# TensorE's layer loop begins with the scores, and the waits of the groups behind them stand ahead of them

## What is computed

```python
def attn_layer(x, Wqkv, qs, ksc, Wo):            # 16 heads of 64, window of 32 tokens
    q, k, v = jnp.split(x @ Wqkv, 3, -1)         # after heads are split:
    q = l2norm(q) * qs; k = l2norm(k) * ksc
    q = q * cos * scale + rotate_half(q) * sin * scale
    k = k * cos / scale + rotate_half(k) * sin / scale
    sim = jnp.einsum('bhwie,bhwje->bhwij', bq, bk2) * 8.0   # own window and the one before
    attn = jax.nn.softmax(jnp.where(mask, -big, sim), -1)
    return jnp.einsum('bhwij,bhwje->bhwie', attn, bv2) @ Wo
for i in range(6):
    x = attn_layer(shift_tokens(x), ...) + x
    x = ffn_layer(shift_tokens(x), ...) + x      # layer norm, W1, a * gelu(gate), W2
```

## Time and profile before

| | us |
|---|---|
| median of three runs | 4279.43 |
| the profiled execution's own time | 4280.44 |
| its span | 4278.5 |
| PE busy | 3922.0 (92%) |
| DVE busy | 3477.7 (81%) |
| ACT busy | 3345.8 (78%) |
| POOL busy | 2759.5 (64%) |
| mean granted clock of TensorE | 0.965 of 2.4 GHz |

### The profile page before, as it was taken

How to read it: one execution, slowest core, us unless ns; L and a number is a source line. 1 busy time by engine, 2 the same in 40 slices (tenths; PEclk the granted TensorE clock), 3 DMA queues, 4 the chain that set the end, 5 groups by cost and what they waited for, 6 DMA issues and landing times. The chain is left out here.

```text
span 4278.5 us, 192301 instructions
## 1 busy us (share of the span) xinstructions
PE 3922.0 (92%) x73440; PEld 3294.1 (77%) x73441; DVE 3477.7 (81%) x6455; ACT 3345.8 (78%) x6195; POOL 2759.5 (64%) x3194
## 2 busy tenths in 40 slices
PE   6999779866778999999999999999999999999997
PEld 4555437644458888888888888888888888888886
DVE  6888475464568999999989999999999999999994
ACT  4777445543348998999989999899989999899995
POOL 3333146641466777777777777777777777777772
PEclk9999899987879999999999999999999999999999
DMA  4000046447111112211122111311122111221111
GB/s 169 1 0 0 16 137 216 157 139 292 53 46 48 48 47 65 63 47 48 47 77 57 44 46 46 84 50 48 47 68 60 46 48 47 78 57 47 47 44 39
DMA packets 155926, 290.43 MB, mean 68 GB/s; under 512 B 35600, under 2 KB 58256, under 8 KB 152080
## 3 DMA queue, kind: packets, MB, share of 16 engines
q1 hardware_dynamic: 147632, 271.29, 21.5%
q0 software_dynamic: 8192, 17.84, 1.4%
HBM read 87.68 MB, written 62.91 MB: 35 GB/s over the span
## 5 line engine op out<-in xcount | busy, mean ns | idle before, releaser
L2833 POOL TENSOR_TENSOR d_rc<-d_rc,d_rs 128x512 f32<-128x512 f32 x768 | 967.9, 1282 | 277.6 <-DVE d_rs L2900 230.5
L2403 PE MATMUL d_pair<-d_W_parts,d_xs_high 128*128 128x512 f32 x2304 | 782.9, 421 | 71.8 <-issue 37.8
L2843 POOL TENSOR_TENSOR d_rc<-d_rc,d_inv 128x1024 f32<-128x1024 f32 x384 | 723.8, 1906 | 112.0 <-DVE d_inv L2921 111.9
L2650 ACT ACTIVATE d_sq<-d_pair 128x512 f32<-128x512 f32 x768 | 455.5, 593 | 181.4 <-DVE d_rs L2900 118.4
L2900 DVE TENSOR_TENSOR d_rc<-d_pair,d_rot 128x512 f32<-128x512 f32 x768 | 524.2, 683 | 18.0 <-ACT d_sq L2650 11.9
L2900 DVE TENSOR_TENSOR d_rs<-d_pair,d_rot 128x512 f32<-128x512 f32 x768 | 522.1, 680 | 0.0
L2403 PEld LDWEIGHTS d_pair<-d_W_parts,d_xs_high 128*128 128x128 f32 x2304 | 389.9, 191 | 163.5 <-issue 101.9
L2403 PE MATMUL d_pair<-d_W_parts,d_xs_low 128*128 128x512 f32 x1152 | 458.7, 398 | 0.0
L2910 DVE TENSOR_REDUCE d_ss<-d_sq 128x16 f32<-128x1024 f32 x384 | 448.2, 1208 | 0.0
L2928 DVE TENSOR_REDUCE d_mx<-d_pair 128x16 f32<-128x1024 f32 x192 | 235.1, 1225 | 220.5 <-PE d_pair L2489 220.5
L2550 PEld LDWEIGHTS d_pair<-d_OT,d_Wo 128*128 128x128 f32 x3072 | 376.2, 193 | 18.4 <-issue 1.5
(11 more groups left out here) (395 smaller groups left out, 9829.5 us busy)
## 6 DMA issues: line engine op xcount, KB each, us to landing
d_VW<-d_V SPq DMA_DIRECT2D x768, 128.0 KB, 2.4
d_VW<-d_V SPq DMA_DIRECT2D x576, 64.0 KB, 2.0
projection_parts<-b_table SPq DMA_DIRECT2D x36, 512.0 KB, 5.5
d_W_parts<-projection_parts SPq DMA_DIRECT2D x36, 512.0 KB, 5.8
leaf_rows<-a_zeros SPq DMA_DIRECT2D x12, 1152.0 KB, 14.6
q_xrow<-leaf_rows SPq DMA_DIRECT2D x24, 576.0 KB
leaf_out<-q_yrow SPq DMA_DIRECT2D x24, 512.0 KB
b_table<-Wqkv_dram SPq DMA_DIRECT2D x36, 256.0 KB, 5.3
```

The source lines that it names most:

```text
L2403: mm = nc.tensor.matmul(target, x_part[:, t.par, :], W_parts[:, c, w_part, :].bitcast(F32R), start=n == 0, stop=n == 2)
L2650: nc.scalar.activation(sq[:, half, 512 * j:512 * j + 512], ps[:, j, :], ACT.Square).then_inc(s[f"s{qk}{j}_ready"], 1)
L2833: nc.gpsimd.tensor_tensor(own[:, :, a, :], own[:, :, a, :], other[:, :, 1 - a, :], ALU.add).then_inc(s[f"add{qk}_ready"], 1)
L2843: nc.gpsimd.tensor_tensor(heads(rc[:, t.par, half, :]), heads(rc[:, t.par, half, :]), inv[:, t.par, half, :].unsqueeze(2).to_broadcast([12 ...
```

## The change

The slot of TensorE is turned round: scores and attend move from its end to its beginning, one tile index later, so the sequence of groups stays the same except at two points. The first keys product now precedes the second queries product. And the loop's branch, which stood between attend and the products, now stands between `hidden_gate` and scores. All waits of attend, and of the two products behind it those for the weights and for `h_ready`, are put ahead of scores; `xs_split` stays with the first keys product and is dropped from queries 1 and keys 1, which now follow a group that has waited for it.

```diff
-                if t.first:
+                if t.first and what not in ("q1", "k0"):
                     pe.wait_ge(s_w[what], 16 * t.l + 16)
-                wait(pe, "xs_split", t)
+                if what not in ("q1", "k1"):
+                    wait(pe, "xs_split", t)
...
                 if j == 0:
-                    wait(pe, "h_ready", t, -7, HCH)
...
-            def scores(t):
-
-                if not t.live:
-                    return
-                wait(pe, "kt_ready", t)
-                wait(pe, "qt_ready", t)
-                wait(pe, "ot_ready", t, -2)
-                if t.edge:
-                    wait(pe, "sc_ready", t, -1)
+            def needs_of_next_groups(behind, ahead):
+
+                if ahead.live:
+                    if ahead.first:
+                        pe.wait_ge(s_w["k0"], 16 * ahead.l + 16)
+                        pe.wait_ge(s_w["q1"], 16 * ahead.l + 16)
+                    wait(pe, "h_ready", ahead, -7, HCH)
+                if behind.live:
+                    wait_spread(pe, behind)
+                    wait(pe, "pt_ready", behind)
                 pe.sem_inc(s["gate_pe"], 1)
+
+            def scores(t, behind, ahead):
+
+                if t.live:
+                    wait(pe, "kt_ready", t)
+                    wait(pe, "qt_ready", t)
+                    wait(pe, "ot_ready", t, -2)
+                    if t.edge:
+                        wait(pe, "sc_ready", t, -1)
+                needs_of_next_groups(behind, ahead)
+                if not t.live:
+                    return
...
-                wait_spread(pe, t)
-                wait(pe, "pt_ready", t)
-                pe.sem_inc(s["gate_pe"], 1)
...
             def slot(tile):
+                scores(tile(2), behind=tile(3), ahead=tile(0))
+                attend(tile(3))
+                keys(tile(0), 0)
                 queries(tile(0), 1)
-                keys(tile(0), 0)
                 down(tile(7))
...
                 hidden_gate(tile(5))
-                scores(tile(1))
-                attend(tile(2))
```

More of the change, by code:

```diff
@@ L2468, in keys_turned @@
                 turn(kt_pair, lambda hp: rc[:, t.par, 1, hp * 128:hp * 128 + 128], "tk_done")
-            def scores(t):
+            def needs_of_next_groups(behind, ahead):
[7 more added lines that the diff above has]
+                    wait(pe, "pt_ready", behind)
+                pe.sem_inc(s["gate_pe"], 1)
+            def scores(t, behind, ahead):
[6 more added lines that the diff above has]
+                needs_of_next_groups(behind, ahead)
                 if not t.live:
                     return
-                wait(pe, "kt_ready", t)
-                wait(pe, "qt_ready", t)
-                wait(pe, "ot_ready", t, -2)
-                if t.edge:
-                    wait(pe, "sc_ready", t, -1)
-                pe.sem_inc(s["gate_pe"], 1)
                 for odd in range(2):
```

## The result

The changed kernel takes 4309.34 us (median of three runs, 4307.23 to 4318.37), the kernel before 4279.43. The ratio is 1.0076, 95% interval 1.0061 to 1.0091: 26 to 39 us slower, with 4285.5 forecast and 4276 to 4297 as the range. The profiled execution's own time is 4307.23 us.

The account below looks back on a forecast made before the run. TensorE's sequence was taken as the bound, time being won only at its pauses. 4280.44 - 20.4 + 0 + 20 + 4.8 + 2 = 4286.8 us, about 1 less as a median, put at 4285.5; range 4276 to 4297.

Parts of the forecast that it names:

- Steady slots: Loop slots with branch: the shorter pause behind attend gains 0.24 us in each of 85, 20.4 us; none without branch.
- the same limit: Down's wait for VectorE's centred scores, said to hold slots without branch at 15.35 us; with branch they took 15.58.
- The bounds, 10 to 25: Steady-slot gain: 10 us if only the part ahead of down is won, 25 if VectorE's latency is saved too.
- two rivals with other causes: Clock stretches at layer changes, 4296 us, chance 0.27; only half the steady-slot gain, 4296 us, chance 0.13.
- Added waits in steady slots: Scores' new wait for the copy of the turned probabilities, met at the very moment: 0 us, bounds 0 to 4.
- The dropped waits on `xs_split` and the swap cost nothing: Steady slots: dropping the `xs_split` waits and putting the first keys product ahead of queries 1 costs 0 us.
- Changes of layer: At five changes the mask also waits for k0 and q1 weights, late by 4.0 us each: 20 us, nothing given back.
- 22 to 24 us: Length forecast for the slots at the five changes of layer.
- The clock: Half-clock stretches after pauses at layer changes: about four more at 1.2 us each, 4.8 us, bounds 0 and 13.
- The clock rival: Pauses at every layer change cost 1.6 us each, 8 new stretches, 13 us: 4296 us; chance 0.27.
- Straight code: Filling pipeline and drain: scores wait for the copy of the probabilities, 2 us, bounds 0 and 5.
- covers part: Filling pipeline: TensorE's 14.4 us idle ahead of attend was said to cover part of the scores' new waits.

Follow-up runs that it names:

- e4: Kernel before with only the wait for VectorE's rotation put last ahead of values 1, on its first matmul: 4277.81 us, 1.0006.
- e2: Changed kernel with the wait for VectorE's rotation put last ahead of values 1, on its first matmul: 4296.56 us, 1.0041.
- e7: Kernel before with the slot turned round, groups keeping their own waits, and the rotation's wait last ahead of values 1: 4261.88 us, 0.9957.
- e12: e7 with attend's two waits (values spread, turned probabilities) moved ahead of the scores: 4268.40 us, 0.9972.
- e11: Changed kernel with queries 1 ahead of the first keys product again, and `xs_split` waited for by queries 1: 4300.84 us, 1.0055.
- e5: Kernel before with only the first keys product put ahead of the second queries product: 4310.38 us, 1.0072.
- e1: Changed kernel with the waits for the weights of k0 and q1 back at their products: 4286.76 us, 1.0024.
- e3: Changed kernel with attend's two waits (values spread, turned probabilities) back at attend, behind the scores: 4307.85 us, 1.0070.
- e10: Changed kernel with VectorE's two short operations d_norm and d_inv ahead of its row maxima: 4245.49 us, 0.9917.
- e14: e13 with attend's waits at attend in the straight code: 4214.29 us, 0.9851.
- e13: Changed kernel with the edits of e1, e2, e10 and e11 together: 4222.01 us, 0.9870.
- e6: Kernel before with only the slot turned round, every group keeping its own waits, queries before keys: 4274.19 us, 0.9989.
- e8: Changed kernel with the edits of e1 and e2 together: 4270.48 us, 0.9986.
- e9: e7 with VectorE's two short operations d_norm and d_inv ahead of its row maxima: 4242.02 us, 0.9915.

## Why the prediction was wrong

**Steady slots, the step that failed.** The prediction said of a slot with branch: "A slot with branch can fall to the same limit" and "gains 0.23 to 0.24", 20.4 us. It gained 0.05 to 0.06, about 4.6 us in the trace. The first half of the reasoning held: the pause did set that slot (e4), down then waited 0.5 us in both, a slot without branch gained nothing, and the 0.11 us between the centred scores and down stayed. The limit was not the same, though. I checked the first wait behind the pause and took the parity that has no pause as the measure of the other. A second wait four groups behind down, values 1 for the rotation, is fixed to the same end of the scores through the same chain, and in this parity costs 0.2 us more because of the instruction that carries it. The bounds, 10 to 25, had no reason to end at 10: a slot that falls until something else ends last can gain anything from zero. e2 and e7 show that the missing 0.2 us are there (15 and 14 us), and no forecast case named them. The chance of 0.40 for a slower kernel went to two rivals with other causes: that the sign agrees with them is no success of theirs.

**Added waits in steady slots.** 0 us forecast, bounds 0 to 4; in the traces e12 has 0.03 us more than e7 in one parity, 2 to 3 us. Held. "The dropped waits on `xs_split` and the swap cost nothing" is true of the steady slots of the changed kernel (e11) and only there; in the kernel before the swap costs 0.25 us a slot (e5).

**Changes of layer.** 20 us forecast, 19.0 in the trace; the time to the mask from k0's landing was as forecast. I put the pause into the slot behind the mask ("22 to 24 us"), while it counts in the one before; that slot takes 19.1 us at the second change. e1 confirms the sum with the clock: 22 us.

**The clock.** 4.8 us forecast, 4.0 in the slots. The clock rival named its own condition, about five more stretches, and that came: ten of 3.4 us in place of two. Its price did not, since a stretch that starts in the pause lengthened the slot by 0.85 us and not by 1.6. All five kernels that keep the weights' waits ahead of the scores (after, e2, e3, e10, e11) have half-clock rows at five of five changes, with pauses of 3.6 to 5.1 us ahead of the mask. The twelve others, without this pause, have them at one to four of five (two before, four in e7, one in e14), at 1.4 to 1.6 us each (once 2.9), so a difference of 2 to 5 us between two traces can be this alone. The Trainium skill, "TensorE: Matmul & The Clock Gate", section "HAM oscillation — how this bites in real kernels", has each wait for DMA between bursts put the array back on its slow clock. By that rule the trace of after agrees. The pause of before is a wait for VectorE, of which that section doesn't speak.

**Straight code, mis-sized.** 2 us forecast, bounds 0 to 5. The table gives 2.0 + 5.6 + 6.2, 13.7 before rounding, for both ends. The sentence that TensorE's idle time ahead of attend "covers part" was wrong (13.7 of 14.4 us remained). By the traces attend's waits account for 3 to 5 (2.8 between e7 and e12, 4.4 between e3 and after, 5.4 between e14 and e13), the swap for some 7 (e11, 1.3 of them behind the last matmul). That the fill suffers from the swap because ScalarE squares queries 1 first fits the order of its slot, but no run separates it. I had priced the waits by TensorE's idle time alone (3.5 us came out, 0.9 and four smaller were read) and the swap at nothing.

Some 3 us behind the 185th mask appear in every turned kernel, also in e6 and e7. Most of them only changed ends. TensorE's waits from the 185th mask to the end, in before, e6 and after:

```profile
PE d_pair L2522 <- issue: 2.3, 2, 1.8
PE d_pair L2522 <- issue: 4.3, 3, 2.1
PE d_pair L2532 <- issue: 4.0, 3, 1.8
```

Attend's rows pause in the straight code and in the first pass of the loop, and in no later pass. The turned slot puts one attend less ahead of the loop and one more behind it: up to the eleventh mask they pause eight times before (15.8 us) and seven times in e6 (13.8). Over both ends e6 lost nothing against before (276 us each).

**The sum as the runs have it.** Step by step between kernels that differ in one part: turning with the rotation's wait last -18 (e7), attend's waits +6 (e12), swap and `h_ready` +6 (e8), weights' waits +24 (e2), rotation's wait as the program had it +15. That is +33 by the ratios, the measured difference; the steps of 6 are smaller than their uncertainty. By terms of the trace, measured less forecast: steady slots -4.6 against -20.4, changes of layer 19.0 against 20, clock 4.0 against 4.8, straight code 13.7 against 2. The differences are +15.8, -1.0, -0.8 and +11.7, 26 us in sum, where the medians are 24 apart.

## What to carry to other kernels

When a pause goes, follow the slot through every later wait to the point where the next one opens, and measure each distance from the end of its producer to the waiting load, by parity: a wait with hardly any idle time in front of it can still be the next limit, less than 0.1 us behind the first. Compare where the program puts the wait that ends last: here it cost 0.24 us on a sequencer instruction and 0.05 on the matmul. And price a move of waits, of a swap, and of straight code apart: moving a wait ahead of a group makes that group pay for what it didn't need. A change that costs time can still hold a part that gains once another limit has gone (e13 against e9).

## What the runs showed of the hardware

In this kernel a wait that ended last cost 0.05 us from the end of its producer to the weight load where the matmul carried it, and 0.24 us where a register operation (71 ns) carried it and one more wait step followed (rows above). Two products of equal length in the other order cost 31 us in one kernel (e5) and none in the steady slots of another (e11): in the first, ScalarE's squares had 0.4 us to spare ahead of the rotation and came 0.7 later. In straight code attend's matmuls pause for 0.5 to 2.8 us with nothing waited for that the trace shows, behind the loop's first pass not at all; why is open. The clock fell to half at some of the changes of layer in every trace, at one to four of five where nothing but VectorE's tables held TensorE (2.5 us in the kernel before), and at five of five where the mask's pause of some 4 us stood ahead of it.
